# Building the last token lists of a mixture of experts with products in PSUM instead of scatters to memory

## What is computed

```python
    x = x + _L0_attn_ref(_layernorm(x, axis=-1), ...)
    x = x + _L0_ffn_ref(_layernorm(x, axis=-1), ...)
...
        route_logits = jnp.einsum('bsd,de->bse', x, Wr) + br
        routing_weights = jax.nn.softmax(route_logits, axis=-1)
        selected_expert = jnp.argmax(routing_weights, axis=-1)
...
            h = jax.nn.gelu(jnp.einsum('bsd,dh->bsh', x, W1[e]) + b1[e], approximate=False)
            y = jnp.einsum('bsh,hd->bsd', h, W2[e]) + b2[e]
            out = jnp.where((selected_expert == e)[..., None], y, out)
```

## Time and profile before

| | us |
|---|---|
| median of 3 runs | 753.04 |
| fastest and slowest of them | 751.44, 757.42 |
| the profiled execution | 754.28 |
| its span in the profile | 752.5 |
| TensorE busy | 682.8 (91%) |
| VectorE busy | 533.3 (71%) |
| GpSimd busy | 489.3 (65%) |
| ScalarE busy | 470.4 (63%) |

### The profile page before, as it was taken

One profiled execution on the slowest core, in us unless ns is written; L12 is line 12 of the kernel. 1 busy time (PEld: TensorE's weight loads), 2 busy tenths in 40 slices (PEclk: granted clock), 3 DMA queues, 4 the chain that ended last, 5 costly groups with the idle time before them and its releaser, 6 DMA issues.

```text
span 752.5 us, 17346 instructions
## 1 busy us (share of the span) xinstructions
PE 682.8 (91%) x5790; PEld 575.1 (76%) x5791; DVE 533.3 (71%) x907; ACT 470.4 (63%) x983; POOL 489.3 (65%) x611
## 2 busy tenths in 40 slices
PE   8799899998999998997997898749999999999997
PEld 7677677787777776776776778638899999986776
DVE  5899989999999989997889995417443333435441
ACT  3887998998989988887776675303232333324352
POOL 3789988979789878899798684723243433434331
PEclk9699999999999998997999999969999999999999
DMA  7968853343423423743655469241111111111010
GB/s 239 298 202 261 265 167 101 87 136 106 148 85 107 142 72 99 131 71 111 103 98 60 139 195 329 14 36 51 57 50 56 59 49 51 49 43 39 25 43 15
DMA packets 43999, 82.59 MB, mean 110 GB/s; under 512 B 5896, under 2 KB 14349, under 8 KB 43920
## 3 DMA queue, kind: packets, MB, share of 16 engines
q1 hardware_dynamic: 38288, 68.97, 32.1%
q0 software_dynamic: 5632, 12.61, 6.8%
HBM read 69.62 MB, written 13.52 MB: 110 GB/s over the span
## 4 chain that ended last, share of the span: by engine, by line
PE 58%; POOL 12%; issue 11%; ACT 10%; DVE 4%; DMA 3%; DVEq 1%; POOLq 0%; ACTq 0%; SPq 0%
PE WW L1155 13%; PE misc L1192 13%; PE WW L1032 11%; PE YY L1070 8%; POOL w_sb L650 7%; ACT w_sb L829 4%; ACT Csb L819 4%; DMA bcd<-token_rows,gcol 2%; PE misc L1187 2%; POOL lists L656 2%; PE WW L1149 2%; PE misc L958 2%; POOL b_sb L631 2%; PE misc L970 1%; DMA xin<-x_in 1%
## 5 line engine op out<-in xcount | busy, mean ns | idle before, releaser
L650 POOL TENSOR_TENSOR w_sb<-w_sb,Csb 128x512 f32<-128x512 f32 x202 | 254.9, 1272 | 57.3 <-DVE w_sb L1283 49.3
L1032 PE MATMUL WW<-b_sb,xin 64*128 64x130 f32 (+2 forms) x2304 | 203.5, 294 | 28.2 <-DVE w_sb L1283 14.5
L1032 PEld LDWEIGHTS WW<-b_sb,xin 64*128 64x128 f32 x2304 | 169.1, 193 | 75.7 <-issue 36.4
L1283 DVE TENSOR_TENSOR_SCAN w_sb<-WW,hlast,w_sb 128x512 f32<-128x512 f32 x152 | 187.6, 1269 | 9.4 <-issue 5.0
L829 ACT ACTIVATE w_sb<-dt,negA 128x512 f32<-128x512 f32 x256 | 169.8, 709 | 8.9 <-DVE w_sb L1283 5.8
L905 ACT ACTIVATE dt<-WW,b1c 128x128 f32<-128x128 f32 x256 | 72.9, 387 | 151.5 <-PE WW L1155 149.3
L1070 PE MATMUL YY<-sm,w_sb 128*128 128x128 f32 x1024 | 143.8, 286 | 8.6 <-DVE row L1340 8.6
L723 POOL DMA_INDIRECT y_out<-CbX,ocol x36 | 42.1, 1171 | 144.0 <-DVE CbX L1675 138.6
L1070 PEld LDWEIGHTS YY<-sm,w_sb 128*128 128x128 f32 x1024 | 114.8, 145 | 23.4 <-POOL w_sb L650 7.6
L1192 PE MATMUL misc<-w_sb,dt 128*128 x512 | 117.3, 383 | 0.3 <-issue 0.3
L819 ACT ACTIVATE Csb<-w_sb,invA 128x512 f32<-128x512 f32 x134 | 91.6, 713 | 27.8 <-POOL w_sb L650 27.6
(11 more groups left out here) (271 smaller groups left out, 850.8 us busy)
## 6 DMA issues: line engine op xcount, KB each, us to landing
w_sb<-c_rows SPq DMA_DIRECT2D x86, 256.0 KB, 4.0
CbX<-c_rows SPq DMA_DIRECT2D x42, 256.0 KB, 3.6
w_sb<-w_in SPq DMA_DIRECT2D x20, 512.0 KB, 6.5
token_rows<-row SPq DMA_DIRECT2D x8, 1024.0 KB
w_sb<-w_in SPq DMA_DIRECT2D x24, 256.0 KB, 5.5
xin<-x_in SPq DMA_DIRECT2D x8, 512.0 KB, 3.9
w_sb<-x_in SPq DMA_DIRECT2D x7, 512.0 KB, 9.1
b_sb<-b_in SPq DMA_DIRECT2D x1, 780.0 KB, 6.7
```

The source lines that it names most:

```text
L650: eng.tensor_tensor(hc[g % NHC], hb_of(g), Csb[i % NCS][:, :], ALU.mult).then_inc(s_hcp, 1)
L1032: return eng.matmul(to[:, a:a + width], x_rows[rows, k, h * P:(h + 1) * P], band[rows, k, at:at + width], start=start, stop=not start, ski ...
L1283: eng.tensor_tensor_scan(hb_of(g) if pooled(g) else w_of(g), w_of(g), A[g % NA], hlast[(q - 1) % 2][:, h * N + n:h * N + n + 1] if q % NC ...
```

## The change

Batches 1 and 2 are no longer scattered to `lists` and read back. For each row tile VectorE computes, from the slots, a column (which of the 256 list columns) and a row in it. It writes three marks in bf16 by comparing a counting row `counted` (0, 1, 2, ...) with these: two of 128 columns, of which one holds, where the row matches, a number for the lane (4096 minus the token of row tile 31) and the other 128 times (31 minus row tile), and one of 256 columns that is 1 where the column matches. TensorE multiplies the 128-column marks with the 256-column one and sums over all row tiles of the batch in one bank (hop `spread`). The sum at a listed place is 4096 minus the row number, and 0 elsewhere. `join` subtracts it from the lists so far (`listed`), in which an empty place holds 4096 (FAR is now 4096). The hop `shift` is one product with the identity that moves the lower 64 partitions of the list to the upper ones; before, this came from the reload.

The core of the diff:

```diff
-            def enlist(batch, tiles):
-
-                wait_alone(eng, s_slot, batch + 1, s_pconst)
+            def enlist(tiles):
+
+                wait_alone(eng, s_slot, 1, s_pconst)
...
                 if isinstance(t, int) and t == 0:
                     rstd(1, NQ)
-                    eng.wait_ge(s_lists, 16)
-                    enlist(1, range(16, 28))
-                if isinstance(t, int) and t == 2:
-                    enlist(2, range(28, NT))
                 put(t, u)
...
             refill_rings()
             store_rows(NQ - 1)
-            load_lists(1)
...
-                    if q:
-                        for i in range(E * CAP // P):
-                            at = E * CAP + i * P
-                            mm = eng.transpose(to[:, at:at + P], z[1][:, i * P:(i + 1) * P], ident)
+                elif name == "spread":
+                    tiles = (BATCHES[q][1] - BATCHES[q][0]) * TI
+                    done = (BATCHES[q][0] - BATCHES[1][0]) * TI
+                    for j in range(tiles):
+                        eng.wait_ge(s_mark, done + j + 1)
+                        for part in range(2):
+                            mm = eng.matmul(to[:, 0:E * CAP], mark_p[j][:, part, :], mark_c[j],
+                                            start=(j == 0 and part == 0), stop=(j == tiles - 1 and part == 1))
+                elif name == "shift":
+                    wait_read(eng, "spread", 2)
+                    mm = eng.matmul(to[HALF:P, 0:E * CAP], ident[0:HALF, 0:HALF], listed[0:HALF, :],
+                                    start=True, stop=True)
...
                 if isinstance(t, int) and t == 1:
-                    wait_read(eng, "rank", NQ - 2)
+                    wait_read(eng, "spread", 1)
...
                     for hop in TAIL[1:5]:
                         fill(*hop)
                         keep_warm(6)
+                    fill("spread", 1)
                 outputs(t, u)
...
                 if isinstance(t, int) and t == 1:
                     fill("rank", NQ - 1)
+                if isinstance(t, int) and t == 2:
+                    fill("spread", 2)
                 if isinstance(t, int) and t == 4:
-                    fill("lists", 1)
+                    fill("shift", 0)
...
-                eng.tensor_copy(slotu[:, q0 * TI:q1 * TI], slotf).then_inc(s_slot, 1)
+                if batch == 0:
+                    eng.tensor_copy(slotu[:, :], slotf).then_inc(s_slot, 1)
+                    return
+                row_at, column, sum_at = (where[:, i, 0:tiles] for i in range(3))
+                done(eng.tensor_scalar(sum_at, slotf, 1.0 / P, -(P - 1) / (2.0 * P), ALU.mult, ALU.add), "rt")
+                done(eng.tensor_scalar(column, sum_at, ROUND, None, ALU.add), "rt")
+                done(eng.tensor_scalar(column, column, ROUND, None, ALU.subtract), "rt")
+                eng.scalar_tensor_tensor(row_at, column, float(-P), slotf, ALU.mult, ALU.add).then_inc(s_slot, 1)
+                eng.wait_ge(s_slot, batch + 1)
+                for j in range(tiles):
+                    k = q0 * TI + j
+                    eng.tensor_scalar(mark_p[j][:, 0, :], counted[:, 0:P], row_at[:, j:j + 1], lane[:, :],
+                                      ALU.is_equal, ALU.mult)
+                    eng.tensor_scalar(mark_p[j][:, 1, :], counted[:, 0:P], row_at[:, j:j + 1], float(P * (NT - 1 - k)),
+                                      ALU.is_equal, ALU.mult)
+                    eng.tensor_scalar(mark_c[j], counted[:, :], column[:, j:j + 1], None,
+                                      ALU.is_equal).then_inc(s_mark, 1)
+
+            def count():
+
+                done(eng.memset(counts, 1.0), "rt")
+                done(eng.tensor_tensor_scan(counts, counts, counts, -1.0, ALU.mult, ALU.add), "rt")
+                done(eng.tensor_copy(counted[:, :], counts), "rt")
+                done(eng.tensor_scalar(lane[:, :], col("tok0", NT - 1, NT), -1.0, float(ROWS), ALU.mult, ALU.add), "rt")
+
+            def join(batch):
+
+                if batch == 1:
+                    eng.wait_ge(s_store, 16 * NQ)
+                    wait_read(eng, "xnr1", NQ - 1)
+                    done(eng.tensor_copy(listed, ids[:, 0:E * CAP]), "rt")
+                else:
+                    eng.wait_ge(s_spread, 1)
+                eng.wait_ge(s_full, HOP["spread", batch] + 1)
+                eng.tensor_tensor(listed, listed, spot("spread", batch)[:, 0:E * CAP], ALU.subtract)\
+                   .then_inc(s_spread, 1)
...
             aggregate(1, q)
+            eng.wait_ge(s_ids, 1)
+            count()
...
                     for part in range(4):
                         choose(2, part)
+                    join(1)
...
                     last_table()
+                    join(2)
...
                 if isinstance(t, int) and t == 4:
-                    keep_ids(1)
+                    eng.wait_ge(s_gcol, SURE)
+                    eng.wait_ge(s_full, HOP["shift", 0] + 1)
+                    eng.tensor_copy(ids[HALF:P, FAR_A + 1:FAR_B], spot("shift", 0)[HALF:P, 0:E * CAP])
+                    eng.tensor_copy(ids[:, 0:E * CAP], listed).then_inc(s_ids, 1)
```

More of the change, by code:

```diff
@@ L47 @@
 ENTRIES = FULL + 2 * len(SPLIT)
+ROUND = float(2 ** 23)
 SURE = -(-(BATCHES[0][1] * TC - E * (P - 1)) // P)
@@ L53 @@
 FAR_A, FAR_B = E * CAP, 2 * E * CAP + 1
-FAR = 1.0e6
+FAR = float(ROWS)
 EPS = 1e-5
@@ L71 @@
 SOON = 4
-ODD = ("u01", "xn0", "bcd", "dt2_0", "dt2_1", "rank")
+ODD = ("u01", "xn0", "bcd", "dt2_0", "dt2_1", "rank", "spread")
 PARTS = ("bcd_a", "u_a")
-UNEVACUATED = ("u01", "u23", "route", "rank", "lists", "turn") + PARTS
-LATE = (("xnr0", NQ - 1), ("xnr1", NQ - 1), ("routeT", NQ - 1), ("route", NQ - 1), ("rank", NQ - 1), ("lists", 1))
+UNEVACUATED = ("u01", "u23", "route", "rank", "lists", "spread", "shift", "turn") + PARTS
+LATE = (("xnr0", NQ - 1), ("xnr1", NQ - 1), ("routeT", NQ - 1), ("route", NQ - 1), ("rank", NQ - 1), ("spread", 2),
+        ("shift", 0))
 def hops(q):
@@ L92, in hops @@
     return at
-TAIL = (("rank", BATCHES[1][1] - 1),) + LATE
+TAIL = (("rank", BATCHES[1][1] - 1),) + LATE[:4] + (("spread", 1),) + LATE[4:]
 HOP, BANK, BEFORE, READ = {}, {}, {}, {}
@@ L110 @@
         READ[_hop] = ("ids", _q + 1)
+    elif _name in ("spread", "shift"):
+        READ[_hop] = ("spread", _q if _name == "spread" else len(BATCHES))
     elif _name == "turn":
@@ L337, in build @@
         ids = sb("ids", [P, FAR_B + 1], U32)
+        most = max(b - a for a, b in BATCHES[1:]) * TI
+        listed = row[:, 0, 0:E * CAP]
+        counts = tail[:, 0:E * CAP]
+        counted = sb("counted", [P, E * CAP], BF16)
+        where = sb("where", [P, 3, most])
+        lane = sb("lane", [P, 1])
+        spare = sm[:, OFF["wcd"][0]:OFF["skip"][1]]
+        kept = [(spare[:, 0:P], spare[:, P:2 * P]), (spare[:, 2 * P:3 * P], spare[:, 3 * P:4 * P]),
+                (brow[0][:, :, :].rearrange("p i n -> p (i n)"), brow[1][:, :, :].rearrange("p i n -> p (i n)")),
+                (cbrow[:, :, :].rearrange("p i n -> p (i n)"), z[1][:, TC - P:TC])]
+        lent = [(some[:, 2 * i * P:(2 * i + 1) * P], some[:, (2 * i + 1) * P:(2 * i + 2) * P])
+                for some in (CbX, tail) for i in range(4)]
+        mark_p = [p.bitcast(BF16).rearrange("p (a c) -> p a c", c=P) for p, _ in kept + lent]
+        mark_c = [c.bitcast(BF16) for _, c in kept + lent]
         WW = ps("WW", [P, NW * 512])
@@ L415, in build @@
         s_lists = sem("lists_loaded")
+        s_mark = sem("tokens_marked")
+        s_spread = sem("spread_read")
         s_ids = sem("lists_turned_kept")
@@ L440, in build @@
         read_by = {"free": s_free, "freev": s_freev, "dt": s_dt, "lg": s_lg, "slot": s_slot,
-                   "ids": s_ids, "xT": s_xT}
+                   "ids": s_ids, "xT": s_xT, "spread": s_spread}
         def wait_read(eng, name, q):
@@ L511, in load_weights, with load_lists @@
                     eng.dma_start(w2_sb[:, a:a + H], w2[:, a:a + H]).then_inc(s_w2a, 16)
[L513 to L517, removed]
+            def load_lists():
+                eng.wait_ge(s_scat, 16 * TI * BATCHES[0][1])
                 eng.dma_start(lists_in.rearrange("p (a c) -> p a c", c=P),
@@ L682, in emit @@
                     if q == NQ - 3 and n > 4 and n % 2:
-                        enlist(0, ((n - 5) // 2,))
+                        enlist(((n - 5) // 2,))
                     if q == NQ - 2 and n % 2:
-                        enlist(0, ((n + 11) // 2,))
+                        enlist(((n + 11) // 2,))
                     if last and n < 2:
-                        enlist(0, (n + 14,))
+                        enlist((n + 14,))
                     if last and n in (8, 10, 13):
@@ L1450, in first_table, with keep_ids @@
                     eng.tensor_tensor(tile_cu[:, 0:SURE], tc, kth, ALU.add).then_inc(s_first, 1)
[L1452 to L1459, removed]
+            def keep_ids():
+                eng.wait_ge(s_full, HOP["lists", 0] + 1)
```

(1 more changed line is left out.)

6 lines of the change are left out of this document (3 added, 3 removed).

## The result

The changed kernel took 741.42 us (median, 739.52 to 744.60), the kernel before 752.96 in the same series: ratio 0.985, 95% interval 0.981 to 0.989. Two later series, each on another chip, gave 0.988 (0.983 to 0.993) and 0.987 (0.984 to 0.990). It is faster by 1.2 to 1.5%, and the median lies 1.6 us from the forecast of 743. The profiled execution took 739.52 us with a span of 737.8.

What follows compares the result with a forecast made beforehand. It took TensorE's 15.47 us wait for gather(4), queued behind slow scatters, as the bound. 17.5 us gained, less 1.5 (count), 2.0 (clock) and 2.6 + 0.9 (products), gives 10.5, so 743 us; range 738.5 to 748.5.

Steps and rivals of the forecast that it cites:

- (a): Before turn_x(4): without the scatters gather(4) lands in 3.4 us; 15.5 us of idle TensorE and 2.0 of low clock go.
- 1. count(): On VectorE before copy_W1(2): count() adds 1.5 us, all on the path, so hidden(2) starts later.
- 2. The clock: At hidden(2): 3.65 us of idle TensorE most likely drops the clock from 2.4 to 1.2 GHz, costing 2.0 us.
- 3. Marks: On VectorE: 0.73 us a tile, 8.8 for twelve, hidden under the hops except at the end; spread(1) products 2.6 us.
- The rival of cheap marks: VectorE's marks run at the rate of the f32 copies or better, 0.46 us a tile: 741.6 us; chance 0.12.
- 4 and 5: Behind the marks: join and finish(0) stay off the path; gather(4) is hidden with 0.8 us to spare; spread(2) adds 0.9.
- 6: Expert tiles behind finish(1): VectorE sets the pace, hidden(5) starts at 502.8, hidden(6) at 510.8 instead of 521.3, 10.5 us gained.

Runs made afterwards that it cites:

- before_rows512: The kernel before, with the sixteen scatters of its last two batches writing 512-byte rows to another tensor instead of 4-byte numbers; 742.17 us, ratio 0.990.
- back16: The changed kernel with the sixteen scatters of batches 1 and 2 given back at their old places, their output unread; 752.20 us, ratio 1.003.
- before_again: The unchanged kernel before, profiled once more; 750.56 us (one).
- marks_twice: The changed kernel with each of the twelve mark tiles of batch 1 made twice; 750.73 us, ratio 0.999.

## Why the prediction was right, step by step

**(a)** The stall went: turn_x(4) waited 15.47 us before and not at all after, and gather(4) landed in 3.5 us (3.4 forecast). The cause, 4-byte writes at 18 ns each with put(0) and gather(4) queued behind them, is shown by before_rows512. That the scatters as such carry the whole gain is shown by back16. What I did not see is that with the scatters readers of TensorE's products also start late, and that the row I subtracted was one pattern of two. So the close fit is in part luck. Against before_again the changed kernel is 6.1 to 7.1 us ahead at hidden(8), against the profile that I had 10.0 to 11.0, and the medians of the three series 7.5, 10.0 and 11.5. My 10.5 lies among them, but nothing in my working says how often each pattern comes. My steps, which only take a wait for gather(4) and the clock behind it away, would have found 2.02 us of it in the other profile, less than the new work costs, and so no gain.

**1. count()** 1.5 forecast, 1.63 measured (hidden(2) at 4.07 for 2.44).

**2. The clock.** Idle time 3.79 (3.65 forecast), then 0.50, cost 1.64 (2.0 forecast, 1.64 to 2.70 in three profiles). The inference from one row, that 2.15 us of idle time keep it, was too good: in before_again the same 2.15 us were followed by 0.50 and 5.27 us for hidden(2). So a part of this cost may be no cost of the change. The stretch behind that idle time in before_again:

```profile
466.00:468.00 2.00, 2.00 (x11) 0.51 0.73 278
```

**3. Marks.** 0.58 us a tile for 0.73, 7.0 for 8.8: the start of a 128-column mark with two pointers to the next mark is 0.23 us, of one with one pointer 0.17, of a 256-column one 0.19. I had 0.20, 0.20 and 0.33. From 128 to 256 columns only 0.03 us are added. That is four elements a cycle, as the table of the Trainium skill's page "VectorE: DVE Perf Modes" (The perf-mode tier table) has it, and the trace agrees there; but the part that doesn't depend on the width was 0.13 us with one pointer and 0.19 with two, so that a tile took 0.58 us and not the 0.32 worked out from the page. I had overlooked that this page of the Trainium skill (The TRN2 errata) itself calls the formula too short and gives a measured fixed part of about 150 cycles at 0.96 GHz; an estimate with that is 0.60 us a tile, and the trace agrees. My reading that the f32 row ran at one element a cycle was most likely wrong too: if the 0.19 us of two pointers are taken off, its 0.33 us leave 0.14 for 256 columns, and that is two elements a cycle, as the same table has it. spread(1) took 2.62 us, forecast 2.6, spread(2) 0.87 for 0.9. (The rival of cheap marks is 741.9 by its own terms, 743 less 1.1, not 741.6; nothing else hangs on it.)

**4 and 5.** Logits(7) followed the last mark without a gap, join(1) waited 0.33 us for spread(1), and gather(4) was in time. All stayed off the path.

**6.** VectorE was not the pace at hidden(5): TensorE did not wait there (1 to 2 us forecast; 0.82 before). Marks cheaper by 0.15 us a tile are part of that. hidden(6) gained 11.4 us, forecast 10.5: 17.1 for (a), less 1.63, 1.64, 2.62 and 0.87, and 0.8 of VectorE's with 0.3 in small pieces. By hidden(8) 0.4 of it was lost again to a longer wait for VectorE (1.71 us for 1.34).

## What to carry to other kernels

Scattering small numbers to memory cost far more here than its issue: count the writes, look for the last signal and not the last issue, and look at which engines wait "remote" meanwhile. Before subtracting a stall of one profile, take a second profile: the same work can lose much of its time in other places, and then removing the stall alone brings less. On-chip products are a good substitute where they lie under a wait, but VectorE's share becomes path once TensorE waits for it, and idle TensorE behind it can pay once more in clock (2.8 us in marks_twice).

## What the runs showed that I had not expected

- Indirect scatters of 128 four-byte elements, one issued each 1.26 us, were signalled done at 17.7 ns a write (twelve of them; 20 ns with nine); 512-byte rows kept up with the issue.
- While nine or twelve of them were issued, a finished product's reader on ScalarE or VectorE started 4 to 7 us late in six of seven profiles, with rows of either width, with marks or without. The last such wait ended 1.3 to 2.3 us behind the last of twelve scatters, and 0.1 us behind the last of nine. The changed kernels had none of it. What holds these readers up isn't settled, nor why the profile of before was spared.
- The granted clock fell after 2.15 us of idle TensorE in one execution and held in two others; after 2.50 and 3.8 us it fell in each.
